# ScalarE rounds Wo's chunks 53 and 54 ahead of the last head pair's exponentials

## The reference, cut to what matters

```python
q2 = (q @ wiq.T + biq).reshape(N, H, D).transpose(1, 0, 2)      # k2, v2 likewise
scores = jnp.einsum('hnd,hmd->hnm', q2, k2) * scale + mask[None]
attn = jax.nn.softmax(scores, axis=-1)
out = jnp.einsum('hnm,hmd->hnd', attn, v2)
out = out.transpose(1, 0, 2).reshape(N, OUT_F)
return out @ wo.T + bo
# then: x = x + that; layernorm; fake-quantised gate, up, silu, down; x = x + that
```

## Time and profile before

| | |
|---|---|
| median of 3 runs | 333.87 us (333.7, 333.87, 337.89) |
| the profiled execution: its time | 334.12 us |
| its span, first to last instruction | 332.4 us |
| mean granted TensorE clock | 0.996 |
| PE busy | 321.8 us, 97% of the span |
| DVE, POOL, ACT busy | 67%, 57%, 55% of the span |
| the last head pair and the output projection | about 260 to 304 us of the span |

### The profile page before, as it was taken

How to read it: one execution, slowest core, us unless ns; L and a number is a source line. 1 busy time by engine, 2 the same in 40 slices (tenths; PEclk the granted TensorE clock), 3 DMA queues, 4 the chain that set the end, 5 groups by cost and what they waited for, 6 DMA issues and landing times.

```text
span 332.4 us, 5966 instructions
## 1 busy us (share of the span) xinstructions
PE 321.8 (97%) x2071; PEld 295.9 (89%) x2072; DVE 223.1 (67%) x597; ACT 181.9 (55%) x332; POOL 190.0 (57%) x259
## 2 busy tenths in 40 slices
PE   5999999999999999999999999999999999999993
PEld 5899998878999999999999999999999878888852
DVE  3857898856255554753185978879797776497573
ACT  3847357464333333333375968677595866244562
POOL 6686678557777767679816493564727757100004
PEclk9999999999999999999999999999999999999998
DMA  7997334658234333483412241303214120000005
GB/s 256 374 405 280 126 129 160 222 188 241 67 121 129 128 126 127 126 330 123 142 63 66 64 141 50 128 6 123 63 64 128 58 72 0 0 2 0 2 0 191
DMA packets 16827, 41.72 MB, mean 126 GB/s; under 512 B 3504, under 2 KB 7456, under 8 KB 16800
## 3 DMA queue, kind: packets, MB, share of 16 engines
q1 hardware_dynamic: 13088, 38.08, 33.4%
q0 software_dynamic: 2064, 1.80, 2.0%
q10 hardware_dynamic: 1648, 1.48, 1.3%
HBM read 37.99 MB, written 3.37 MB: 124 GB/s over the span
## 4 chain that ended last, share of the span: by engine, by line
PE 88%; DVE 4%; ACT 3%; DMA 2%; issue 1%; POOL 1%; SPq 0%; DVEq 0%; ACTq 0%
PE PS L776 65%; PE PS L933 5%; PE PS L921 5%; PE PS L909 4%; PE PS L1072 2%; DMA X<-in_x 1%; DMA V<-in_w_down 1%; PE PS L845 1%; PE PS L835 1%; PE PS L767 1%; PE PS L820 1%; PE PS L839 1%; POOL QT L468 1%; PE PS L810 1%; PE PS L757 1%
## 5 line engine op out<-in xcount | busy, mean ns | idle before, releaser
L430 POOL TENSOR_TENSOR ring<-stage,ring 128x256 fp32r<-128x256 f32 x124 | 90.6, 767 | 41.6 <-ACT ring L519 38.5
L776 PE MATMUL PS<-XT,ring 128*128 128x384 f32 x528 | 93.5, 336 | 0.0
L776 PEld LDWEIGHTS PS<-XT,ring 128*128 128x128 f32 x528 | 91.4, 188 | 0.4 <-DVE AT L1236 0.3
L448 POOL DMA_INDIRECT codes<-ecol,place x51 | 58.9, 1155 | 25.3 <-issue 16.9
L519 ACT ACTIVATE ring<-stage 128x1024 fp32r<-128x1024 f32 x52 | 54.3, 1057 | 5.8 <-DMA stage<-in_weights 1.9
L626 ACT ACTIVATE scratch<-scratch,smx 128x384 f32<-128x384 f32 x48 | 28.9, 605 | 18.5 <-DVE smx L1370 18.5
L776 PE MATMUL PS<-QT,ring 128*128 128x384 f32 x192 | 35.5, 338 | 0.0
L776 PE MATMUL PS<-AT,ring 128*128 128x384 f32 x192 | 35.2, 338 | 0.0
L776 PEld LDWEIGHTS PS<-AT,ring 128*128 128x128 f32 x192 | 33.0, 188 | 1.5 <-issue 1.5
L776 PE MATMUL PS<-ring,AT 128*128 128x512 f32 x144 | 34.0, 393 | 0.0
L1274 DVE TENSOR_TENSOR ring<-stage,ring 128x1024 fp32r<-128x1024 f32 x21 | 25.7, 1227 | 12.1 <-issue 7.4
(11 more groups left out here) (202 smaller groups left out, 479.0 us busy)
## 6 DMA issues: line engine op xcount, KB each, us to landing
stage<-in_weights SPq DMA_DIRECT2D x56, 512.0 KB
V<-in_w_gate_up SPq DMA_DIRECT2D x4, 512.0 KB, 7.2
codes<-scratch SPq DMA_DIRECT2D x3, 576.0 KB, 14.5
X<-in_x SPq DMA_DIRECT2D x3, 512.0 KB, 5.1
scratch<-codes POOLq DMA_DIRECT2D x2, 576.0 KB, 5.7
scratch<-in_w_gate_up SPq DMA_DIRECT2D x2, 512.0 KB
V<-in_w_down SPq DMA_DIRECT2D x5, 176.0 KB, 5.2
codes<-ecol,place POOLq DMA_INDIRECT x51
```

Of the source, the lines that this page charges most:

```text
L430: ins = pool.tensor_tensor(ring[1][:, slot, piece], stage[:, slot % STAGE, piece], ring[0][:, slot, piece].bitcast(F32), ALU.subtract)
L448: pool.indirect_dma_start(codes[b].rearrange("(n a) -> n a", a=1), bass.IndirectOffsetOnAxis(ap=place[:, t:t + 1], axis=0), ecol[:, VAL, t ...
L776: ins = pe.matmul(outs, lhs[a], rhs[b], start=start and n == 0, stop=stop and n == 2, skip_group_check=True)
```

## The change

Four lines move in ACT's list, and nothing else is edited. Ahead of `exps(7, 0)` now stand three `spare_high` in a row (52, 53, 54); `spare_high(55)` stands where 53 stood, between `o_take(6, 1)` and `probs_high(7, 0)`; nothing stands any more between `probs_high(7, 1)` and the two last `o_take`.

```diff
@@ -680,15 +680,15 @@
             pair_high(51)
             o_take(6, 0)
             spare_high(52)
+            spare_high(53)
+            spare_high(54)
             exps(7, 0)
             exps(7, 1)
             o_take(6, 1)
-            spare_high(53)
+            spare_high(55)
             probs_high(7, 0)
             probs_high(7, 1)
-            spare_high(54)
             o_take(7, 0)
-            spare_high(55)
             o_take(7, 1)
```

## The result

| | before | changed |
|---|---|---|
| median | 333.87 us | 340.64 us (5 runs, 339.25 to 341.78) |
| ratio, with its 95% interval | | 1.0187, 1.0156 to 1.0218 |
| span of the profiled execution | 332.4 us | 338.7 us |
| mean granted clock | 0.996 | 0.988 |

A forecast was written before the change was run, and what follows sets the result against it. The prediction took PE, busy for 97% of the span, to bound the kernel. PE's wait +4.9, the clock +2.3 and the saved wait -0.3 summed to +6.9 us, giving 340.8 us, with a range of 334.5 to 342.0.

The forecast's parts named there:

- The collision: Last pair, first head: three POOL subtractions and DVE's three multiplications take whole turns; p_ready at 278.57 in place of 272.37.
- the prediction's list of signs: What would show it right or wrong, such as multiplications of about 2.3, 2.2 and 2.2 us ending near 278.6.
- The wait of PE: PE's transposes for the last pair's first head start at 278.65 in place of 273.73: +4.9 us.
- The clock: PE's idle 4.9 us drops the granted clock to 0.5; half of the low stretch is lost: +2.3 us.
- the wait for DVE's low parts: PE waits 0.3 and 0.2 us at turn_probs(7, 1): +0.5 us, hidden if the clock falls.
- What the change gives: PE's wait ahead of chunk 54's six matmuls, at 281.37, goes: -0.3 us.
- The clock's fall: A PE gap of 4.9 us makes the clock fall, 7 in 10, from one fall 2.0 us after PE's last matmul.
- case 2: Rival: DVE and POOL take turns but the clock stays up: +5.1 us, 339.0; chance 0.2.
- Case 3: Rival: DVE's first-head multiplications wait only once or twice, then keep POOL off: 334.9 or 337.2; chance 0.18.
- Cases 4 and 5: Rivals: no collision, 0.3 us faster, 333.6, chance 0.1; or chunk 54 lands late, holding back the exponentials, chance 0.05.
- The bound: Two per cent slower, 340.55 us; chances given: faster 0.01, same 0.68, slower 0.31.
- case 1: Likeliest: DVE and POOL take turns and the clock falls: +6.9 us, 340.8, own range 340.1 to 341.5; chance 0.47.

The follow-up runs named there:

- e3: Changed kernel with only the copy of 53 ahead of the exponentials, 54 and 55 back where they stood before: 335.33 us, ratio 1.0039 to the kernel before.
- e6: Changed kernel with the copy of 55 moved back between the last two o_take, so two low parts stand ready: 337.49 us, ratio 1.0101 to the kernel before.
- e2: Changed kernel with each low part of 52 to 55 made in four short GpSimd instructions in place of one: 334.69 us, ratio 1.0041 to the kernel before.
- e5: Changed kernel with line 1383's multiplications of the last pair also summing their output into a spare column: 334.13 us, ratio 1.002 to the kernel before.
- e7: Kernel before, ScalarE's list untouched, plus two unread GpSimd subtractions right behind pair_v(7): 341.33 us, ratio 1.0218 to the kernel before.
- e4: Changed kernel with 70 dummy matmuls in TensorE's gap, between output(1, 0) and turn_probs(7, 0): 338.18 us, ratio 1.0115 to the kernel before.
- e0: Changed kernel as it is, run again as reference beside three others on the same chip: 340.2 us, ratio 1.0176 to the kernel before.
- e8: Changed kernel with GpSimd waiting for the first head's p_ready, so its three subtractions lie on the second head's multiplications: 340.97 us, ratio 1.0212 to the kernel before.
- e1: Changed kernel with GpSimd held until the last pair's second head is normalised: 333.37 us over 12 runs, ratio 0.9989 to the kernel before.

## Why the prediction was right

**The collision** was read from two pairs of rows in another part of the trace (rows 7 to 9) and carried over to the last pair. Its steps held one by one: POOL first by 0.3 us; multiplications of 2.31, 2.51 and 2.49 us where the working has 2.30, 2.57 and 2.57 (the prediction's list of signs has 2.3, 2.2 and 2.2, which does not follow from its own times); end at 278.37 for 278.57. That one subtraction of 2.4 us holds as whole as a piece of 0.7 was the part that no row showed; e3, e6 and the changed kernel count it off, e2 shows that length is what matters, e5 and e7 that nothing else is needed.

**The terms.** The wait of PE: +4.9 forecast, +4.8 measured. The clock: +2.3 forecast, +2.2 measured (+2.1 with the 0.08 us above set against it), and it did hide the wait for DVE's low parts, which e4 brought to light with 0.4 for my 0.5. What the change gives: -0.3 forecast, -0.5 measured; I compared six matmuls that are followed by another kind of work (1.47 us), while the six ahead of chunk 54 run on into their like at 1.38. Sum +6.9 against +6.4 by the rows; 340.8 against a median of 340.64. That the median came within 0.2 us is partly luck: the profiled execution was 6.3 us above the one before (340.44 against 334.12), and the same kernel in the first set of experiments 6.0 us by the medians (e0).

**How the clock's price was come by.** The 2.3 us rest on the pitch of PE's first matmuls, 111 against 60 ns, read as the low level. The trace of before doesn't show that level there; its granted clock reads 1.00 in the very stretch of the slow pitch:

```profile
4.00:5.00 1.00, 1.00 (x12) 1.00 (x11) 0.19 (x1) 0.90 (x2) 0.52 (x3) 1.00 1.06 416
```

So this step of the working had no support in the clock's own column, and its agreement with the measured 2.2 doesn't bear that reading out. The price is shown by the changed kernel's rows and by e4.

**The clock's fall** was given 7 in 10 on the strength of one row at the kernel's end. It fell in all five profiled executions with a gap of 2.5 us or more that was left idle (the changed kernel, e0, e6, e7, e8), and also behind the 2.0 us in e5, so my case 2 was seen in none. Case 3, which was to have DVE's run of three keep POOL off, is contradicted: POOL took its turn between them each time. Cases 4 and 5 didn't come: the exponentials started at 269.06.

**The bound.** Two per cent lay at 340.55, inside case 1's own range (340.2 to 341.4 by its terms; the 340.1 and 341.5 of the prediction are a little wide), and the interval of the ratio crosses it; that the split of the chances between "within" and "over" was nearly even within case 1 was fair.

## What to carry to other kernels

Before an engine's work is pulled forward, ask what it releases on the engines behind it: here the two copies were free on ScalarE, and their cost was three GpSimd subtractions that now lay on VectorE's multiplications, at 2.0 us each on a path with 1.4 us of slack. GpSimd's idle time in the old kernel was no waste but the cover of that path, so hold the released work with a wait on the sensitive step (e1), or cut it into short instructions (e2, which still left 1.0 us of loss). Where TensorE's wait can't be avoided, dummy matmuls in it keep its clock up; they gave back 2.0 of 6.0 us (e4).

## What the runs showed of the hardware

- The two engines took strict turns wherever rows show both waiting, with POOL's instructions of 2.4 us and with pieces of 0.7 us (e2): neither had two instructions in a row, and the three multiplications took about 1.1, 3.0, 5.1 and 7.1 us beside none, one, two and three subtractions.
- The sum-writing form of the multiplication is slower alone (0.61 against 0.41 us) and is not held.
- The granted clock fell 2.2 to 3.2 us after TensorE's last matmul, in six executions with idle time of 2.0 (e5), 2.5 (e6), 3.7 (e8) and 4.6 us (the changed kernel, e0, e7); in e5 TensorE was already at work again when it fell. It stayed up behind idle times of 0.45 (e3), 0.68 (e4) and 1.03 us (e2). It was then low for 3.1 (e6) to 5.1 us (e7) of work without a wait, 4.6 us in the changed kernel.
